# Layer 1 of a four-layer graph network: eight row steps of VectorE spread over the step, and the first product ahead of the scan

## The chip, the cores and the metric

The kernel runs on one core of one Trainium2 chip, as one launch. The metric is device time in microseconds (us), the median of three runs. The core has five engines with queues of their own: TensorE (PE in the profile, PEld for its weight loads), VectorE (DVE), ScalarE (ACT), GpSimd (POOL) and SyncE (SP, which only starts transfers). They meet at semaphores. An engine works through its queue in order, so a wait holds everything behind it on that engine.

## The reference, cut to what matters

Four graph layers run one after the other over 3125 nodes of 64 features and 100,000 edges, sorted by destination. A layer norm of the sum of input and layer output ends each of them. The change touches only the edge stage of layer 1:

```
q     = (x @ Wq)                       # nodes x 8 heads x 16
x_dst = x[edge gather]                 # 64 features per edge
k     = wk * sum_s sh[:, s] * (x_dst @ Cqk[:, s, :])     # s = 0..8
v     = wv * sum_s sh[:, s] * (x_dst @ Cv[:, s, :])
attn  = sum over 16 of q[node] * k     # 8 logits per edge
alpha = softmax of attn over the edges of one node
upd   = segment_sum(v * alpha)
```

The node of `q`, of the softmax and of the sum is the one by which the edges are sorted. The edges of one node are therefore neighbours, and softmax and sums are done as scans.

## The kernel before, in words

Each of the 128 partitions holds a run of 784 neighbouring edges, taken eight at a time (`C = 8`). So layer 1 has `NCH = 98` steps, one for each eight columns, and `edges_1` holds the queues of all engines for them. Nearly every buffer is a pair, chosen by the parity of the step. VectorE and TensorE run steps in a loop of two (`chunks`; its first four and last two steps stand outside the loop on VectorE). GpSimd, ScalarE and SyncE have all 98 steps written out (`all_chunks`). Inside the loop a semaphore is compared with a number worked out from the loop's register.

In one step t the engines do this:

- **SyncE** loads `SHB` (the factors sh, 1 MB), `SH_LAST` (512 KB), `WKV` (wk and wv, 1 MB) and `Q` (`spread_q`, 512 KB), in this order, each behind the waits that tell that its buffer is free. `Q` holds the q row only at the first edge of each node and zero elsewhere.
- **GpSimd** issues eight indirect gathers of source rows (line 1315, tile `G`), one for each column. Between columns 3 and 4 stand two tensor instructions: `messages` (line 1300, `MSG` = v times weight, for the step four earlier in its own order) and `low_part` (line 1292, `LAST`). `messages` waits for `args_ready` of the step after its own.
- **TensorE** turns the gathered rows (line 1334, `XT`; needs all eight gathers) and then makes eight columns (lines 1348 to 1352, `COLS`). Its order is column 0 of step t, the turn of step t+1, columns 1 to 7 of step t. `col_done` rises behind column 3 and behind column 7.
- **VectorE** makes from `XT` and the factors the operands `LAST` (line 1433) and `XF` (line 1435) of step t+1. `product` (line 1444) multiplies one half of `COLS` by `WKV`. `expand_q` (line 1457) fills `Q`: row j is row j of `Q` plus `SAME_HERE` times row j-1, eight dependent instructions. `ask` (line 1468) multiplies the first half of `WKV` by `Q`. `logits` (lines 1476, 796, 800, 802, 804) reduces to logits, scans the running maximum and makes the arguments of the exponentials. `sums` (line 1491) is the scan of the messages, 1224 elements long.
- **ScalarE** does the exponentials, the decay factors, the split of `LAST` in two parts (`high`, `split`) around `low_part`, and the stores of scanned rows.

VectorE's order in step t is second product of t-1, logits of t-1, LAST and XF of t+1, sums of t-2, first product of t, the eight row steps of t+1, ask of t+1.

For the operands that matter below: `XT` and `COLS` lie in PSUM, and so LAST, XF and the products read one tensor from SBUF. The row steps, ask, the maximum scan, the three argument instructions and the scan of `sums` read two tensors from SBUF. `messages` and `low_part` read two from SBUF on GpSimd.

Of the kernel before, what the change touches and what calls it, by code (L numbers as in the profile page):

```python
# [18 lines left out]
ALU = mybir.AluOpType  # L19
ACT = mybir.ActivationFunctionType  # L20
AX = mybir.AxisListType
# [6 lines left out]
C = 8  # L28
J = 784
NCH = J // C  # L30
# [3 lines left out]
CH = 16  # L34
# [21 lines left out]
def graph_kernel(nc, x, dst_shifted, src, ea16t, ea64t, ea9t, etype, ew, w64, we8, cfix, w1, w2, b1, b2, wout, vecs, basis,  # L56
# [16 lines left out]
    spread_q = dram("spread_q", [EPAD, 128])  # L73
# [10 lines left out]
    with top:  # L84
# [49 lines left out]
        class Steps:  # L134
# [10 lines left out]
            def wait(self, back=0):  # L145
                self.eng.wait_ge(self.sem, self.base + (self.n - back))
# [1078 lines left out]
        def edges_1(src_ap):  # L1225

            with ExitStack() as ctx:
                e = Edges(ctx, 1, [(x1_tab, 128, "src")], {"src": src_ap})
                WKV = e.pair("WKV", [P, C, 256])
                Q = e.pair("Q", [P, C, 128])  # L1230
                FIRST_Q = sb("FIRST_Q", [P, 128], F32, ctx)
                SRC = sb("SRC", [P, J], I32, ctx)
                SAME_HERE = e.pair("SAME_HERE", [P, C])
                SHB, XF = e.pair("SHB", [P, 4, C * P]), e.pair("XF", [P, 4, C * P])
                SH_LAST, LAST = sb("SH_LAST", [P, C * P], F32, ctx), sb("LAST", [P, C * P], F32, ctx)
                RW = e.pair("RW", [P, C, 256])
# [15 lines left out]
                asked, weighted = e.sem("asked"), e.sem("weighted")  # L1252

                with nc.Block() as block:
                    @block.sync
                    def _(sp):
                        sp.dma_start(SRC[:, :], src_ap).then_inc(src_in, 16)
                        sp.dma_start(CF[:, :, :], cfix[0:4 * P, :].rearrange("(k p) n -> p k n", p=P))\
                          .then_inc(w_in, 16)
                        sp.dma_start(CF_LAST, cfix[4 * P:5 * P, :]).then_inc(w_in, 16)  # L1260

                        def step(t, n, b, first, last):
                            if not first:
                                wait(sp, made, t * 2 - 2)
                            for h in range(2):
                                sp.dma_start(SHB[b][h:P:2, :, :].rearrange("p k n -> p (k n)"),
                                             ea9t[bass.ds(t, 1), h, 0:4 * C * P].to_broadcast([64, 4 * C * P]))\
                                  .then_inc(sh_in[b], 16)
                            if not first:
                                wait(sp, made, t * 2 - 1)  # L1270
                            sp.dma_start(SH_LAST[:, :], ea9t[bass.ds(t, 1), 0, 4 * C * P:5 * C * P]
                                         .to_broadcast([P, C * P])).then_inc(last_in, 16)
                            if not first:
                                wait(sp, col_used, t * 2 - 2)
                            sp.dma_start(WKV[b][:, :, :], row_view(wkv_tab, t)).then_inc(wkv_in[b], 16)
                            if not first:
                                wait(sp, q_expanded, t)
                                wait(sp, asked, t - 1)
                            sp.dma_start(Q[b][:, :, :], row_view(spread_q, t)).then_inc(q_in[b], 16)
                        all_chunks(step)  # L1280

                    @block.gpsimd
# [133 lines left out]
                    def _(v):  # L1416
# [8 lines left out]
                        def outer(t, n, b, first):  # L1425

                            wait(v, sh_in[b], (n + 1) * 32)
                            if not first:
# [5 lines left out]
                              .then_inc(made, 1)  # L1434
                            nc.vector.tensor_tensor(XF[b][:, 0:4, :], XT[:, :].unsqueeze(1).to_broadcast([P, 4, C * P]),  # L1435
                                                    SHB[b][:, 0:4, :], ALU.mult).then_inc(made, 1)
# [11 lines left out]
                        def expand_q(t, n, b, first):  # L1448

                            st = Steps(v, q_steps, t * (C - 1))  # L1450
                            if first:
                                wait(v, first_q_in, 16)
                            wait(v, q_in[b], (n + 1) * 16)
                            wait(v, flagged, t + 1)
                            row = FIRST_Q[:, :] if first else Q[1 - b][:, C - 1, :]
                            for j in range(C):
                                ins = nc.vector.scalar_tensor_tensor(out=Q[b][:, j, :], in0=row,  # L1457
                                                                     scalar=SAME_HERE[b][:, j:j + 1],
                                                                     in1=Q[b][:, j, :], op0=ALU.mult, op1=ALU.add)
                                row = Q[b][:, j, :]  # L1460
                                if j < C - 1:
                                    st.then(ins)
                            ins.then_inc(q_expanded, 1)

                        def ask(t, n, b):
                            wait(v, wkv_in[b], (n + 1) * 16)
# [1 line left out]
                            nc.vector.tensor_tensor(WKV[b][:, :, 0:128], WKV[b][:, :, 0:128], Q[b][:, :, :], ALU.mult)\  # L1468
                              .then_inc(asked, 1)

                        def logits(t, n, b, first):
                            st = Steps(v, e.a_steps, t * 4)
                            wait(v, col_used, (t + 1) * 2)
                            if not first:
                                wait(v, e.args_ready, t)
                            st.do(nc.vector.tensor_reduce(e.LG[:, :, 1:1 + C].rearrange("p h j -> p j h"),
                                                          RW[b][:, :, 0:128].rearrange("p j (h c) -> p j h c", c=CH),
                                                          AX.X, ALU.add))
                            wait(v, broken, t + 1)
                            e.maxima(v, st, t, n, b, first)  # L1480
                            assert st.n == 4, st.n

                        def sums(t, n, b, first):
                            wait(v, e.decays_ready, t * 2 + 2)
# [9 lines left out]
                            wait(v, e.scanned, t + 1)  # L1494

                        def step(t, n, b, first, last):
                            if first:
                                expand_q(0, 0, 0, True)
                                ask(0, 0, 0)
                                outer(0, 0, 0, True)  # L1500
# [12 lines left out]
                        end = NCH - 1  # L1513
                        product(end, NCH // 2 - 1, 1, 1)
                        logits(end, NCH // 2 - 1, 1, False)
# [490 lines left out]
```

## Time and profile before

| what | value |
|---|---|
| median of three runs | 5541.78 us |
| the three runs | 5535.75, 5542.93, 5541.78 us |
| profiled execution, its own time | 5538.3 us |
| its span | 5536.5 us |
| PE, DVE, ACT, POOL busy, share of span | 49%, 67%, 35%, 72% |
| layer 1's edge stage, steady steps | 1405.42 to 3070.77 us of the span |

The shares are means over stages of different kinds. The stretch in the last row is 92 whole steps, from the start of one LAST instruction of VectorE to that of another 92 steps later. A row of the timeline begins with start and duration in us, then engine, line, operation, output<-inputs and shapes; in brackets stand the idle time of the engine before it and what ended it. Two instructions can overlap in time on VectorE: the next may start before the recorded end of the one before.

### The profile page before, as it was taken

Reading aid. Unit: us, or ns where it says so; the run is one execution under the profiler, and the core shown is the slowest. Engines: PE = TensorE matmul, PEld = TensorE weight load, DVE = VectorE, ACT = ScalarE, POOL = GpSimd, SP = SyncE. Lnnn points to the kernel's source line nnn. Section 1 sums busy time; section 2 is a strip of 40 time slices with the busy share of each in tenths; the row PEclk is TensorE's granted clock in tenths of the full one; section 3 lists DMA queues with packets and bytes.
Section 4 is the critical chain, followed back from the end, with each engine's and each line's share of the span. In section 5 each row is a group of like instructions: output and inputs, shape, how many; then the busy total and the mean of one; then the engine's idle time right before and its main releaser. Section 6 shows DMA issues by size and latency. Waiting matters only on the chain. (4 is left out here: it accounts for less than half of the span.)

```text
span 5536.5 us, 48725 instructions
## 1 busy us (share of the span) xinstructions
PE 2686.0 (49%) x12353; PEld 2156.0 (39%) x12353; DVE 3714.6 (67%) x5208; ACT 1939.4 (35%) x3077; POOL 4005.5 (72%) x3569
## 2 busy tenths in 40 slices
PE   1777776745999999999999530000001610000001
PEld 0444444434888888888888530000000410000001
DVE  3888888864999999999999656666665532222223
ACT  0666666641333333333333222222222311111111
POOL 4777777755888888888888457777776057777774
PEclk8899989977999999999999755555555865555555
DMA  7777777745777777777778333333333632222221
GB/s 287 251 259 259 256 257 258 257 154 207 299 286 298 294 286 299 291 290 300 292 289 301 114 90 107 109 106 107 108 107 88 282 138 55 53 55 55 53 55 44
DMA packets 393535, 1064.64 MB, mean 192 GB/s; under 512 B 140390, under 2 KB 163490, under 8 KB 352228
## 3 DMA queue, kind: packets, MB, share of 16 engines
q1 hardware_dynamic: 229156, 753.21, 36.8%
q0 software_dynamic: 107840, 167.64, 11.8%
q10 hardware_dynamic: 56448, 142.93, 6.8%
q14 instruction: 76, 0.62, 0.0%
q8 instruction: 15, 0.25, 0.0%
HBM read 671.77 MB, written 391.75 MB: 192 GB/s over the span
## 5 line engine op out<-in xcount | busy, mean ns | idle before, releaser
L1348 PE MATMUL COLS<-CF,XF 128*128 128x256 f32 x6272 | 1490.2, 381 | 8.0 <-DVE XF L1435 7.5
L1348 PEld LDWEIGHTS COLS<-CF,XF 128*128 128x128 f32 x6272 | 1140.0, 191 | 131.4 <-DVE XF L1435 7.9
L1315 POOL DMA_INDIRECT G<-x_tab,SRC x784 | 1016.6, 1297 | 233.4 <-issue 203.1
L772 POOL DMA_INDIRECT G<-rel_tab,IDX_rel x784 | 739.8, 944 | 387.0 <-issue 249.0
L1615 PE MATMUL CP<-IDENT,LROW 128*68 128x128 f32 (+1 forms) x12 | 3.4, 422 | 2041.9 <-DVE SM L1736 2041.9
L772 POOL DMA_INDIRECT G<-xl_tab,IDX_src x784 | 778.1, 992 | 259.1 <-issue 249.7
L886 ACT ACTIVATE OUT<-SC 128x576 f32<-128x576 f32 (+3 forms) x392 | 572.6, 1461 | 1073.2 <-DVE SC L832 914.2
L772 POOL DMA_INDIRECT G<-kv_tab,IDX_src x784 | 739.7, 943 | 250.6 <-issue 249.7
L1615 PEld LDWEIGHTS CP<-IDENT,LROW 128*68 128x68 f32 (+1 forms) x12 | 1.5, 158 | 2042.9 <-DVE SM L1736 2042.8
L825 DVE TENSOR_TENSOR MSG<-G,EW 128x512 f32<-128x512 f32 x98 | 100.0, 1020 | 733.8 <-DMA G<-rel_tab,IDX_rel 724.6
L996 PE MATMUL WK<-W,HT 128*128 128x256 f32 x1568 | 451.0, 415 | 0.0
L1435 DVE TENSOR_TENSOR XF<-XT,SHB 128x4096 f32<-128x4096 f32 x98 | 432.7, 4415 | 0.0
L1351 PE MATMUL COLS<-CF_HI,X 128*128 128x256 f32 x784 | 366.9, 468 | 0.0
L993 PE MATMUL WK<-B2R,ONER 128*128 128x512 f32 x392 | 229.6, 586 | 271.8 <-ACT WKV L1044 270.1
L996 PEld LDWEIGHTS WK<-W,HT 128*128 128x128 f32 x1568 | 329.0, 210 | 53.7
L853 ACT ACTIVATE EX<-ARG 128x64 f32<-128x64 f32 (+1 forms) x196 | 55.5, 283 | 808.5 <-DVE ARG L804 808.5
L1491 DVE TENSOR_TENSOR_SCAN SC<-DEC,MSG 128x1224 f32<-128x1224 f32 x98 | 321.7, 3282 | 12.9 <-POOL MSG L1300 9.3
L1300 POOL TENSOR_TENSOR MSG<-RW,EX 128x1024 f32<-128x1024 f32 x98 | 284.5, 2903 | 27.1 <-DVE ARG L804 22.4
L1457 DVE SCALAR_TENSOR_TENSOR Q<-Q,SAME_HERE 128x128 f32<-128x128 f32 x783 | 274.7, 351 | 24.3
L832 DVE TENSOR_TENSOR_SCAN SC<-DEC,MSG 128x612 f32<-128x612 f32 (+1 forms) x196 | 272.6, 1391 | 14.9
L1161 DVE TENSOR_TENSOR T<-G,XE 128x512 f32<-128x512 f32 x98 | 67.4, 688 | 313.8 <-DMA G<-kv_tab,IDX_src 313.8
L1444 DVE TENSOR_TENSOR RW<-COLS,WKV 128x1024 f32<-128x1024 f32 x196 | 239.4, 1221 | 19.0 <-PE COLS L1352 7.3
(252 smaller groups left out, 5685.5 us busy)
## 6 DMA issues: line engine op xcount, KB each, us to landing
SHB<-ea9t SPq DMA_DIRECT2D x196, 1024.0 KB, 9.9
wkv_tab<-WKV SPq DMA_DIRECT2D x98, 1024.0 KB, 7.6
WKV<-wkv_tab SPq DMA_DIRECT2D x98, 1024.0 KB, 5.1
scan<-OUT ACTq DMA_DIRECT2D x196, 288.0 KB, 2.5
scan<-OUT ACTq DMA_DIRECT2D x98, 576.0 KB, 2.9
rel_tab<-YS SPq DMA_DIRECT2D x25, 2048.0 KB, 7.4
RAW<-spread SPq DMA_DIRECT2D x196, 256.0 KB
spread_q<-ZQ SPq DMA_DIRECT2D x98, 512.0 KB
```

Source lines behind the costliest of these rows:

```text
L772: pool.indirect_dma_start(out=self.G[g][b][:, c, :], out_offset=None, in_=tab, in_offset=bass.IndirectOffsetOnAxis(ap=self.IDX[which][b][: ...
L832: nc.vector.tensor_tensor_scan(flat(SC[b][:, 0:R, :]), flat(self.DEC[b][:, :, :]), flat(self.MSG[:, :, :]), 0.0, ALU.mult, ALU.add)\
L886: nc.scalar.activation(self.OUT[b][:, :, 0:WD], SC[b][:, 0:WD, 1:1 + C].rearrange("p r j -> p j r"), ACT.Copy).then_inc(self.copied_out, 1)
L996: last = nc.tensor.matmul(WK[:, 512 * i + 256 * a:512 * i + 256 * a + 256], HT[b][:, a, cc * P:(cc + 1) * P], W2[:, :], start=False, stop= ...
L1300: nc.gpsimd.tensor_tensor(e.MSG[:, 0:128, 1:1 + C].rearrange("p (h c) j -> p h c j", c=CH), RW[b][:, :, 128:256].rearrange("p j (h c) -> p ...
L1315: pool.indirect_dma_start(out=e.G[0][b][:, col, :], out_offset=None, in_=x1_tab, in_offset=bass.IndirectOffsetOnAxis(ap=SRC[:, at:at + 1], ...
L1348: nc.tensor.matmul(acc, XF[b][:, k, edges_], CF[:, k, :], start=(k == 0), stop=False)
L1351: nc.tensor.matmul(acc, X4[b][:, edges_], CF_HI[:, :], start=False, stop=False)
L1435: nc.vector.tensor_tensor(XF[b][:, 0:4, :], XT[:, :].unsqueeze(1).to_broadcast([P, 4, C * P]), SHB[b][:, 0:4, :], ALU.mult).then_inc(made, 1)
L1444: nc.vector.tensor_tensor(RW[b][:, four, :], COLS[which][:, :].rearrange("p (c n) -> p c n", c=4), WKV[b][:, four, :], ALU.mult).then_inc( ...
L1457: ins = nc.vector.scalar_tensor_tensor(out=Q[b][:, j, :], in0=row, scalar=SAME_HERE[b][:, j:j + 1], in1=Q[b][:, j, :], op0=ALU.mult, op1=A ...
L1491: nc.vector.tensor_tensor_scan(flat(SC[b][:, 0:136, :]), flat(e.DEC[b][:, :, :]), flat(e.MSG[:, :, :]), 0.0, ALU.mult, ALU.add)\
```

## The change

VectorE's instructions of layer 1 come in another order. `outer` is split in `outer_last` (LAST) and `outer` (XF). `expand_q` becomes `row_step`, of which one is called at a time, and `logits` calls a function `beside` at three places. The one-semaphore chain of `logits` becomes four semaphores. The first product stands ahead of the scan, and takes over a wait for `messages`. SyncE loads `Q` directly behind `SHB`, when row step 0 of the step before is done.

```diff
@@ sync
+                            if not first:
+                                wait(sp, q_steps, (t - 1) * (C - 1) + 1)
+                                wait(sp, asked, t - 1)
+                            sp.dma_start(Q[b][:, :, :], row_view(spread_q, t)).then_inc(q_in[b], 16)
                             if not first:
                                 wait(sp, made, t * 2 - 1)
                             sp.dma_start(SH_LAST[:, :], ea9t[bass.ds(t, 1), 0, 4 * C * P:5 * C * P]
                                          .to_broadcast([P, C * P])).then_inc(last_in, 16)
                             if not first:
                                 wait(sp, col_used, t * 2 - 2)
                             sp.dma_start(WKV[b][:, :, :], row_view(wkv_tab, t)).then_inc(wkv_in[b], 16)
-                            if not first:
-                                wait(sp, q_expanded, t)
-                                wait(sp, asked, t - 1)
-                            sp.dma_start(Q[b][:, :, :], row_view(spread_q, t)).then_inc(q_in[b], 16)
@@ vector
                             if which == 0:
                                 wait(v, asked, t + 1)
+                                if not isinstance(t, int) or t >= 2:
+                                    wait(v, weighted, t - 1)
...
+                        def row_step(t, n, b, j):
+
+                            if j == 0:
+                                wait(v, q_in[b], (n + 1) * 16)
+                                wait(v, flagged, t + 1)
...
+                                    wait(v, q_expanded, t)
+                                    row = Q[1 - b][:, C - 1, :]
+                            else:
+                                wait(v, q_steps, t * (C - 1) + j)
+                                row = Q[b][:, j - 1, :]
...
-                        def logits(t, n, b, first):
-                            st = Steps(v, e.a_steps, t * 4)
+                        def logits(t, n, b, first, beside):
...
+                                                    AX.X, ALU.add).then_inc(reduced, 1)
+                            beside(1)
+                            wait(v, reduced, t + 1)
                             wait(v, broken, t + 1)
...
+                                                         0.0, ALU.add, ALU.max).then_inc(maxed, 1)
+                            beside(2)
+                            wait(v, maxed, t + 1)
...
+                                                    ALU.subtract).then_inc(lowered, 1)
+                            beside(3)
+                            wait(v, fallen, t + 1)
+                            wait(v, lowered, t + 1)
...
                         def step(t, n, b, first, last):
+                            def row(j):
+                                if not last:
+                                    row_step(t + 1, n + b, 1 - b, j)
+
...
                                 product(t - 1, before(n, b), 1 - b, 1)
-                                logits(t - 1, before(n, b), 1 - b, isinstance(t, int) and t == 1)
+                                row(0)
+                                logits(t - 1, before(n, b), 1 - b, isinstance(t, int) and t == 1, row)
+                            row(4)
                             if not last:
-                                outer(t + 1, n + b, 1 - b, isinstance(t, int) and t == 0)
+                                outer_last(t + 1)
+                                outer(n + b, 1 - b)
+                            product(t, n, b, 0)
+                            row(5)
                             if not isinstance(t, int) or t >= 2:
                                 sums(t - 2, n - 1, b, isinstance(t, int) and t == 2)
-                            product(t, n, b, 0)
+                            row(6)
+                            row(7)
                             if not last:
-                                expand_q(t + 1, n + b, 1 - b, False)
                                 ask(t + 1, n + b, 1 - b)
```

## Rows read from the trace of the kernel before

**Rows 1.** Busy time by stretch: length, PE, PEld, DVE, ACT, POOL, PEclk, DMA share, GB/s.
```profile
1405.42:3070.77 1665.35, 1549.73 (x8097) 1380.02 (x8096) 1583.15 (x1749) 633.17 (x1012) 1442.38 (x917) 1.00 0.78 293
```
**Rows 2.** Timeline of VectorE, one step: start, duration, engine, line, operation.
```profile
2199.53 1.22 DVE L1476 TENSOR_REDUCE LG<-RW 128x64 f32<-128x1024 f32 x1
2200.88 0.31 DVE L796 TENSOR_TENSOR_SCAN SC<-BR,LG 128x72 f32<-128x72 f32 x1
2201.22 0.23 DVE L800 TENSOR_TENSOR ARG<-SC 128x64 f32<-128x64 f32 x1
2201.36 0.22 DVE L802 TENSOR_TENSOR ARG<-LG,SC 128x64 f32<-128x64 f32 x1
2201.62 0.23 DVE L804 TENSOR_TENSOR ARG<-ARG,BR 128x64 f32<-128x64 f32 x1
...
2202.09 1.23 DVE L1433 TENSOR_TENSOR LAST<-XT,SH_LAST 128x1024 f32<-128x1024 f32 x1 [0.24 <-issue]
...
2203.23 4.42 DVE L1435 TENSOR_TENSOR XF<-XT,SHB 128x4096 f32<-128x4096 f32 x1
...
2207.56 3.18 DVE L1491 TENSOR_TENSOR_SCAN SC<-DEC,MSG 128x1224 f32<-128x1224 f32 x1
...
2210.86 1.23 DVE L1444 TENSOR_TENSOR RW<-COLS,WKV 128x1024 f32<-128x1024 f32 x1
...
2212.00 3.06 DVE L1457 SCALAR_TENSOR_TENSOR Q<-Q,SAME_HERE 128x128 f32<-128x128 f32 x8
...
2215.16 1.23 DVE L1468 TENSOR_TENSOR WKV<-WKV,Q 128x1024 f32<-128x1024 f32 x1
...
2216.30 1.22 DVE L1444 TENSOR_TENSOR RW<-COLS,WKV 128x1024 f32<-128x1024 f32 x1
```
**Rows 3.** Groups of VectorE over 92 steps: xcount, busy us, mean ns, idle before.
```profile
L1491 DVE TENSOR_TENSOR_SCAN SC<-DEC,MSG 128x1224 f32<-128x1224 f32 x92 | 304.6, 3311 | 0.0
```
**Rows 4.** Timeline of GpSimd, the same step.
```profile
2202.93 2.92 POOL L1300 TENSOR_TENSOR MSG<-RW,EX 128x1024 f32<-128x1024 f32 x1
...
2205.78 2.39 POOL L1292 TENSOR_TENSOR LAST<-LAST,X 128x1024 f32<-128x1024 f32 x1
...
2208.32 3.21 POOL L1315 DMA_INDIRECT G<-x_tab,SRC  x1 [0.16 <-issue]
...
2214.34 0.94 POOL L1315 DMA_INDIRECT G<-x_tab,SRC  x1 [0.30 <-issue]
...
2215.59 1.62 POOL L1315 DMA_INDIRECT G<-x_tab,SRC  x1 [0.30 <-issue]
...
2220.01 0.94 POOL L1315 DMA_INDIRECT G<-x_tab,SRC  x1 [0.30 <-DVE ARG L804]
```
**Rows 5.** Timeline of an early step: low_part ends before the scan starts.
```profile
1373.09 2.38 POOL L1292 TENSOR_TENSOR LAST<-LAST,X 128x1024 f32<-128x1024 f32 x1
...
1375.49 2.70 DVE L1491 TENSOR_TENSOR_SCAN SC<-DEC,MSG 128x1224 f32<-128x1224 f32 x1
...
1375.61 3.38 POOL L1315 DMA_INDIRECT G<-x_tab,SRC  x1
```
**Rows 6.** Timeline of TensorE: the turn, the last matmul of columns 3 and 7.
```profile
2216.96 1.09 PE L1334 MATMUL XT<-IDENT,G 128*128 128x128 f32 x8 [1.21 <-DMA G<-x_tab,SRC]
...
2223.66 0.28 PE L1352 MATMUL COLS<-CF_LO,X 128*128 128x256 f32 x1
...
2231.51 0.28 PE L1352 MATMUL COLS<-CF_LO,X 128*128 128x256 f32 x1
```
**Rows 7.** Timeline: VectorE instructions and gathers that start close together, twice.
```profile
1362.81 0.94 POOL L1315 DMA_INDIRECT G<-x_tab,SRC  x1 [0.30 <-issue]
...
1363.23 1.22 DVE L1468 TENSOR_TENSOR WKV<-WKV,Q 128x1024 f32<-128x1024 f32 x1
...
2309.08 0.38 DVE L796 TENSOR_TENSOR_SCAN SC<-BR,LG 128x72 f32<-128x72 f32 x1
...
2309.12 0.94 POOL L1315 DMA_INDIRECT G<-x_tab,SRC  x1 [1.74 <-issue]
```
**Rows 8.** SyncE's load of Q: its issue, and over 92 steps the time to landing.
```profile
2217.99 0.35 SPq L1279 DMA_DIRECT2D Q<-spread_q  x1
...
DMA to landing us min/median/max: 5.6/6.2/6.8
```
**Rows 9.** Timeline of TensorE, two turns of early steps.
```profile
1351.69 1.04 PE L1334 MATMUL XT<-IDENT,G 128*128 128x128 f32 x8
...
1368.28 1.03 PE L1334 MATMUL XT<-IDENT,G 128*128 128x128 f32 x8
```
**Rows 10.** Timeline of VectorE in an early step, outside the loop.
```profile
1369.82 0.23 DVE L804 TENSOR_TENSOR ARG<-ARG,BR 128x64 f32<-128x64 f32 x1
1370.02 1.23 DVE L1433 TENSOR_TENSOR LAST<-XT,SH_LAST 128x1024 f32<-128x1024 f32 x1
```

More of the change, by code:

```diff
@@ L1252, in edges_1 @@
                 asked, weighted = e.sem("asked"), e.sem("weighted")
+                reduced, maxed = e.sem("reduced"), e.sem("maxed")
+                fallen, lowered = e.sem("fallen"), e.sem("lowered")
                 with nc.Block() as block:
@@ L1423, in _, with outer_last @@
                           .then_inc(cf_lo, 1)
-                        def outer(t, n, b, first):
-                            wait(v, sh_in[b], (n + 1) * 32)
-                            if not first:
+                        def outer_last(t):
+                            if not isinstance(t, int) or t > 0:
                                 wait(v, col_done, t * 2 - 2)
@@ L1434, in outer @@
                               .then_inc(made, 1)
+                        def outer(n, b):
+                            wait(v, sh_in[b], (n + 1) * 32)
                             nc.vector.tensor_tensor(XF[b][:, 0:4, :], XT[:, :].unsqueeze(1).to_broadcast([P, 4, C * P]),
@@ L1446, in product @@
                                                     WKV[b][:, four, :], ALU.mult).then_inc(col_used, 1)
[L1448 to L1463, printed above, removed]
+                        def row_step(t, n, b, j):
+                            if j == 0:
+                                wait(v, q_in[b], (n + 1) * 16)
+                                wait(v, flagged, t + 1)
+                                if isinstance(t, int) and t == 0:
+                                    wait(v, first_q_in, 16)
+                                    row = FIRST_Q[:, :]
+                                else:
+                                    wait(v, q_expanded, t)
+                                    row = Q[1 - b][:, C - 1, :]
+                            else:
+                                wait(v, q_steps, t * (C - 1) + j)
+                                row = Q[b][:, j - 1, :]
+                            nc.vector.scalar_tensor_tensor(out=Q[b][:, j, :], in0=row, scalar=SAME_HERE[b][:, j:j + 1],
+                                                           in1=Q[b][:, j, :], op0=ALU.mult, op1=ALU.add)\
+                              .then_inc(q_steps if j < C - 1 else q_expanded, 1)
                         def ask(t, n, b):
@@ L1469, in ask @@
                               .then_inc(asked, 1)
[L1471 to L1472 removed]
+                        def logits(t, n, b, first, beside):
+                            flat = lambda ap: ap.rearrange("p h j -> p (h j)")
+                            MS = e.MS[b]
                             wait(v, col_used, (t + 1) * 2)
@@ L1475, in logits @@
                                 wait(v, e.args_ready, t)
-                            st.do(nc.vector.tensor_reduce(e.LG[:, :, 1:1 + C].rearrange("p h j -> p j h"),
-                                                          RW[b][:, :, 0:128].rearrange("p j (h c) -> p j h c", c=CH),
-                                                          AX.X, ALU.add))
-                            wait(v, broken, t + 1)
-                            e.maxima(v, st, t, n, b, first)
-                            assert st.n == 4, st.n
+                            nc.vector.tensor_reduce(e.LG[:, :, 1:1 + C].rearrange("p h j -> p j h"),
+                                                    RW[b][:, :, 0:128].rearrange("p j (h c) -> p j h c", c=CH),
+                                                    AX.X, ALU.add).then_inc(reduced, 1)
+                            beside(1)
+                            wait(v, reduced, t + 1)
+                            wait(v, broken, t + 1)
+                            wait(v, e.max_carried, t)
+                            if not first:
+                                wait(v, e.copied_out, t - 1)
+                            nc.vector.tensor_tensor_scan(flat(MS[:, :, :]), flat(e.BR[:, :, :]), flat(e.LG[:, :, :]),
+                                                         0.0, ALU.add, ALU.max).then_inc(maxed, 1)
+                            beside(2)
+                            wait(v, maxed, t + 1)
+                            if not first:
+                                wait(v, e.exps_ready, t)
+                            nc.vector.tensor_tensor(e.ARG[:, 0, :, :], MS[:, :, 0:C], MS[:, :, 1:1 + C], ALU.subtract)\
+                              .then_inc(fallen, 1)
+                            nc.vector.tensor_tensor(e.ARG[:, 1, :, :], e.LG[:, :, 1:1 + C], MS[:, :, 1:1 + C],
+                                                    ALU.subtract).then_inc(lowered, 1)
+                            beside(3)
+                            wait(v, fallen, t + 1)
+                            wait(v, lowered, t + 1)
+                            nc.vector.tensor_tensor(e.ARG[:, 0, :, :], e.ARG[:, 0, :, :], e.BR[:, :, 1:1 + C], ALU.add)\
+                              .then_inc(e.args_ready, 1)
                         def sums(t, n, b, first):
@@ L1496, in step @@
                         def step(t, n, b, first, last):
+                            def row(j):
+                                if not last:
+                                    row_step(t + 1, n + b, 1 - b, j)
                             if first:
-                                expand_q(0, 0, 0, True)
+                                for j in range(C):
+                                    row_step(0, 0, 0, j)
                                 ask(0, 0, 0)
-                                outer(0, 0, 0, True)
+                                outer_last(0)
+                                outer(0, 0)
+                                for j in range(4):
+                                    row(j)
                             else:
                                 product(t - 1, before(n, b), 1 - b, 1)
-                                logits(t - 1, before(n, b), 1 - b, isinstance(t, int) and t == 1)
+                                row(0)
+                                logits(t - 1, before(n, b), 1 - b, isinstance(t, int) and t == 1, row)
+                            row(4)
                             if not last:
-                                outer(t + 1, n + b, 1 - b, isinstance(t, int) and t == 0)
+                                outer_last(t + 1)
+                                outer(n + b, 1 - b)
+                            product(t, n, b, 0)
+                            row(5)
                             if not isinstance(t, int) or t >= 2:
                                 sums(t - 2, n - 1, b, isinstance(t, int) and t == 2)
-                            product(t, n, b, 0)
+                            row(6)
+                            row(7)
                             if not last:
-                                expand_q(t + 1, n + b, 1 - b, False)
                                 ask(t + 1, n + b, 1 - b)
@@ L1514, in _ @@
                         product(end, NCH // 2 - 1, 1, 1)
-                        logits(end, NCH // 2 - 1, 1, False)
+                        logits(end, NCH // 2 - 1, 1, False, lambda j: None)
                         sums(end - 1, NCH // 2 - 1, 0, False)
```

## The prediction

> **What bounds the kernel now.** I read the busy shares first, and they name no engine: over 92 steady steps of layer 1, VectorE is busy 1583 of 1665 us, TensorE 1550, GpSimd 1442 [rows 1]. The PEclk column is 1.00 there, so TensorE's clock is at its 2.4 GHz level and no term of what follows. A step takes 1665.35 / 92 = 18.10 us.
>
> Then I laid the timelines of VectorE and GpSimd side by side, and they show a cycle through both. VectorE's scan lasts 3.18 us and ends at 2210.74, which is 2.57 behind the end of GpSimd's low_part at 2208.17 [rows 2, 4]. In an early step, where low_part had ended 0.02 before it started, the same scan took 2.70 [rows 5]. Over the 92 steps it averages 3.311 [rows 3]: it waits 0.61 each time. The reverse holds as well. The gather that starts at 2208.32 runs until 2211.53, 0.79 behind the scan's end, where other gathers take 0.94. The gather at 2215.59 ends 0.82 behind the end of ask (2216.39) [rows 2, 4]. So a scan or an ask that is running holds back a gather that starts, and a running low_part holds back the scan.
>
> GpSimd's step follows. Its own work is 0.15 from low_part to the first gather, 7 x 1.25 + 0.94 for eight gathers (0.94 and a gap of 0.30), 0.02, 2.85 from messages to low_part and 2.39 for low_part: 15.10 us. The scan adds 3.21 - 0.94 = 2.27 and ask 1.62 - 0.94 = 0.68 [rows 4]. The sum, 18.05, is the step to 0.05. TensorE isn't the limit: it waits 1.21 us a step for the last gather [rows 6], and turns 16.59 apart when nothing holds it [rows 9].
>
> **The change part by part, in time since product 1 starts.**
>
> *VectorE's path.* Dependent instructions start 0.03 to 0.10 behind the end of the one before (eight row steps take 3.06), independent ones 0.09 ahead of it (XF starts at 2203.23, LAST ends at 2203.32) [rows 2]. A row step of 0.35 therefore costs 0.38 now and 0.26 between strangers. From the reduce to LAST it is 2.56 now; in the new order the starts are 1.13, 0.26, 0.22, 0.26, 0.14, 0.14, 0.26, 0.14, 0.26 apart, 2.81 in all, with four row steps inside. New waits against register values come in: inside the loop five of them let LAST start 0.47 behind the last argument instruction [rows 2], outside it 0.20 [rows 10], about 0.05 each. In the short stretch they may push LAST by 0.1 (bounds 0 and 0.5): 2.9. Ahead of it, product to reduce is 1.40 instead of 1.26. Then LAST to XF 1.14, XF to product 0 4.33, product 0 to row 5 1.14, row 5 to scan 0.26: 11.2 from product 1 to the scan. The scan takes 2.70 if low_part is over, ask starts 0.93 behind its end (0.10 + 0.38 + 0.35 + 0.10), and the next product 1.14 later. VectorE alone would need 11.2 + 2.70 + 0.93 + 1.14 = 16.0 us, against 18.0 now.
>
> A rule of the Trainium skill speaks against this part ("VectorE: DVE Perf Modes", section "The DRAIN you can't avoid"): each instruction starts only when the pipeline has emptied, and leaving a semaphore out gains nothing. By that rule fifteen starts between product 1 and the scan would come 0.09 later each, 11.2 would be 12.55, and the loop worked out below would take 36.2 for two steps: 18.1 a step, no gain. The timeline disagrees, with XF 0.09 ahead of LAST's end; so I leave this a small part of the case "same".
>
> *TensorE.* From turn to the end of column 7 it takes 14.83 [rows 6]. Left alone it would make a step of 16.59 to 16.84 (1549.73 / 92) [rows 1, 9].
>
> *GpSimd, which decides.* Count from the end of low_part as 0. The scan now follows product 0 and row step 5. The first gather starts at 0.15. If the scan starts at 0.2 or later, that gather goes through and the second, due at 1.40, is held until 0.79 behind the scan's end at 2.90: it ends at 3.69 instead of 2.34, 1.35 late. The third starts at 4.00, inside ask (3.83 to 5.06), and ends at 5.88, another 0.94 late. Step: 15.10 + 1.35 + 0.94 = 17.39, and with the 0.05 that the sum above lacks 17.45. The other way round the loop agrees: the last gather ends at 7.13, 1.68 to the turn (2215.28 to 2216.96), 14.83 to column 7, 0.04, then VectorE's 11.2 to the scan: 34.9 for two steps, 17.44 each. VectorE then waits about 1.4 a step for column 7.
>
> Forecast: 18.10 - 17.45 = 0.65 a step, 92 steps, 60 us off the profiled execution's 5538.3 (span and 1.8 around it), which stands 3.5 below the median of the runs. That is 5478; I say **5480**.
>
> *At nothing.* Product 0's new wait for messages: messages end at 2205.85, and product 0 moves to where the scan starts now, 2207.56 [rows 2, 4], 1.7 of slack; behind it would stand row 5, the scan and ask. Column 3 is ready 6.98 behind the turn [rows 6], about then. Q's load is issued now behind WKV's, at 2217.99, lands 6.2 later and is needed at 2230 [rows 2, 8]. Afterwards it is asked for about a step sooner, behind SHB's, and needed about 17 us later. SH_LAST and WKV queue behind it on SyncE, but its wait ends with row step 0, before LAST and about when WKV's buffer is free. Without that cover every late microsecond would be one of VectorE's. The first steps and the layer's end wait for gathers and messages anyway: 0 to 5 us.
>
> **The rivals.**
>
> *Slower: the scan beats the first gather.* If row step 5 and the scan queue up behind low_part, row 5 ends at 0.22 and the scan starts at about 0.13, the gather at 0.15: a photo finish. If the scan has it, the first gather ends at 3.6, the second starts at 3.9 inside ask (3.73 to 4.96), ends at 5.78 instead of 2.34, 3.44 late: 15.10 + 3.44 + 0.05 = 18.6, since scan and ask now stand 0.93 apart where 4.4 lay between them. That is 0.5 x 92 = 46 us worse, 5584. For it: the scan that starts 0.12 ahead of a gather wins [rows 5], and the state keeps itself, since in it VectorE arrives before low_part ends. GpSimd also loses 1.4 us now and then (the idle of 1.74 ahead of one gather [rows 7]), which pushes low_part late. Against it: a scan that starts 0.04 ahead of a gather lost, taking 0.38 instead of 0.31, while the gather took its 0.94; and a gather 0.42 ahead of ask went free [rows 7]. If row steps didn't compete with low_part at all, the scan would take over at 0 and the step be about 18.3, 5560.
>
> The Trainium skill ("SBUF — State Buffer", section "Who interferes with whom") says that whichever of VectorE and GpSimd issues first keeps the shared pair for the whole instruction. It gives no order for a queue behind a third, so it supports either finish.
>
> *Faster: TensorE becomes the bound.* If the gathers slip between scan and ask, GpSimd needs under 16.84 and the step is TensorE's: 1.26 x 92 = 116, 5422. Against it: scan and ask follow each other within less than a gather and its gap (1.25), so both are hit.
>
> *Same.* Steps that alternate between the two finishes, or five short instructions in a row that hold a fourth gather back by 0.6 (17.45 + 0.6): 5535.
>
> **How the numbers follow.** Forecast 0.48, TensorE's bound 0.08, slower 0.34, same 0.10. This kernel's measurement can't tell less than 0.2%, 11 us, from nothing. Faster is 0.56, same 0.10, slower 0.34. The likeliest case alone spans 5455 to 5515 (queue waits 0 to 0.5, 17.2 to 17.85). The range reaches to the slower case and leaves TensorE's bound outside: 5440 to 5592.
>
> **What would show it right or wrong.** Right: the scan at 2.70 instead of 3.31, the first gather behind low_part at 0.94, the second at 2.3, the third at 1.9, a step of 17.4, and an idle of VectorE ahead of product 1 that ends with COLS. Slower case: the first gather at 3.5, the second at 1.9, and row step 5 far above 0.35. If Q's load is late, VectorE idles ahead of row step 0 for a DMA. If LAST starts over 0.6 behind row step 4, the waits in the queue cost more than I allow. The prediction fails if the held gathers together cost GpSimd over 2.95 a step.

## The result and the profile after

The changed kernel takes 5555.14 us, median of 14 runs (5542.88 to 5561.33); the kernel before, run beside it, takes 5543.62 (5535.75 to 5551.03). The ratio is 1.0018 with a 95% interval of 1.0009 to 1.0026: slower by 0.18%, no change by the bound of 0.2%. I had forecast 5480.

The profiled execution is the fastest of the 14: 5542.88 us, span 5541.1. Busy time by stretch over 92 whole steps of it, the columns as in [rows 1], and below that one long step:

```profile
1406.79:3074.25 1667.46, 1555.41 (x8093) 1383.01 (x8092) 1455.75 (x1749) 634.08 (x1013) 1410.58 (x916) 0.98 0.78 293
2056.60:2081.68 25.08, 17.29 (x88) 15.41 (x87) 16.60 (x20) 8.55 (x17) 22.00 (x14) 0.90 0.82 318
```

VectorE is busy 127 us less than in [rows 1], and the 92 steps take 1667.46 instead of 1665.35. Groups of VectorE over the same stretch:

```profile
L1518 DVE TENSOR_TENSOR_SCAN SC<-DEC,MSG 128x1224 f32<-128x1224 f32 x92 | 248.9, 2705 | 0.0
L1451 DVE TENSOR_TENSOR RW<-COLS,WKV 128x1024 f32<-128x1024 f32 x184 | 224.7, 1221 | 135.3 <-PE COLS L1354 127.8 <-POOL MSG L1302 6.2
...
L1434 DVE TENSOR_TENSOR LAST<-XT,SH_LAST 128x1024 f32<-128x1024 f32 x92 | 112.7, 1225 | 52.2 <-PE XT L1336 52.2
```

The scan's 3311 ns [rows 3] have become 2705. VectorE now waits 128 us for columns and 52 us for the turn. The next timelines show that these are two different things. First an ordinary step, GpSimd then VectorE:

```profile
2211.61 0.99 POOL L1317 DMA_INDIRECT G<-x_tab,SRC  x1 [0.16 <-issue]
2212.91 2.20 POOL L1317 DMA_INDIRECT G<-x_tab,SRC  x1 [0.31 <-issue]
2215.41 1.95 POOL L1317 DMA_INDIRECT G<-x_tab,SRC  x1 [0.30 <-issue]
2217.67 0.94 POOL L1317 DMA_INDIRECT G<-x_tab,SRC  x1 [0.30 <-issue]
```
```profile
2201.94 1.22 DVE L1485 TENSOR_REDUCE LG<-RW 128x64 f32<-128x1024 f32 x1
...
2204.77 1.22 DVE L1434 TENSOR_TENSOR LAST<-XT,SH_LAST 128x1024 f32<-128x1024 f32 x1
...
2211.64 2.72 DVE L1518 TENSOR_TENSOR_SCAN SC<-DEC,MSG 128x1224 f32<-128x1224 f32 x1
...
2217.98 1.22 DVE L1451 TENSOR_TENSOR RW<-COLS,WKV 128x1024 f32<-128x1024 f32 x1 [1.43 <-PE COLS L1354]
...
2222.21 1.22 DVE L1434 TENSOR_TENSOR LAST<-XT,SH_LAST 128x1024 f32<-128x1024 f32 x1
```

The step is 2222.21 - 2204.77 = 17.44. The first gather goes through, the second takes 2.20, the third 1.95, and product 1 waits 1.43. This is the forecast state, to the hundredth.

Every 14 steps something else happens, six times in all: GpSimd, VectorE, SyncE and TensorE in the long step of the windows above.

```profile
2056.54 0.94 POOL L1317 DMA_INDIRECT G<-x_tab,SRC  x1 [2.43 <-issue]
...
2062.82 2.37 POOL L1294 TENSOR_TENSOR LAST<-LAST,X 128x1024 f32<-128x1024 f32 x1
2065.35 3.41 POOL L1317 DMA_INDIRECT G<-x_tab,SRC  x1 [0.16 <-issue]
2069.06 1.91 POOL L1317 DMA_INDIRECT G<-x_tab,SRC  x1 [0.30 <-issue]
2071.28 0.95 POOL L1317 DMA_INDIRECT G<-x_tab,SRC  x1 [0.30 <-issue]
2072.53 0.94 POOL L1317 DMA_INDIRECT G<-x_tab,SRC  x1 [0.30 <-issue]
```
```profile
2063.07 1.23 DVE L1451 TENSOR_TENSOR RW<-COLS,WKV 128x1024 f32<-128x1024 f32 x1 [0.91 <-POOL MSG L1302]
2064.21 1.14 DVE L1469 SCALAR_TENSOR_TENSOR Q<-Q,SAME_HERE 128x128 f32<-128x128 f32 x1
2065.27 2.69 DVE L1518 TENSOR_TENSOR_SCAN SC<-DEC,MSG 128x1224 f32<-128x1224 f32 x1
...
2081.68 1.22 DVE L1434 TENSOR_TENSOR LAST<-XT,SH_LAST 128x1024 f32<-128x1024 f32 x1 [7.30 <-PE XT L1336]
```
```profile
2071.32 0.32 SPq L1281 DMA_DIRECT2D WKV<-wkv_tab  x1
2071.68 1.41 SPq L1268 DMA_DIRECT2D SHB<-ea9t  x2
2073.19 0.54 SPq L1274 DMA_DIRECT2D Q<-spread_q  x1
```
```profile
2079.45 1.96 PE L1336 MATMUL XT<-IDENT,G 128*128 128x128 f32 x8 [7.79 <-DMA G<-x_tab,SRC]
```

Read downwards. GpSimd pauses for 2.43 us (such pauses were there before too, at the same gathers, with 1.39 to 1.74 us of idle [rows 7]). Row step 5 is held to the end of low_part (1.14 instead of 0.34), the scan starts 0.08 ahead of the first gather and holds it: 3.41. So the fourth gather ends at 2073.47, and SyncE's loads of 2.5 MB began at 2071.32. The gather's rows land about 6.0 us later (counted to the start of the turn that waits for them), where 2.0 is usual after the change and 1.68 stood in the kernel before. TensorE waits 7.79 and VectorE 7.30. In the ordinary step the fourth gather ended about 0.7 us ahead of the loads, and in the kernel before 2.27 ahead.

The ledger over 92 steps, from the starts of LAST: 6 long steps of 25.51 on average, 6 behind them of 19.05, and 80 others of 17.50. Before, it was 6 of 19.08 at the pauses and 86 of 18.03. The ordinary steps give 80 x 0.53 = 42.6 us back. The long ones cost 6 x (25.51 - 19.08) = 38.6 more than the steps at the pauses did before, and the ones behind them 6 x (19.05 - 18.03) = 6.1: together 44.7. The sum, +2, is what the windows show.

Four of the 80 are 18.4 to 18.6 long, at distances of 17, 17 and 34 steps. In them the fourth gather ended in time, 0.6 to 0.7 us ahead of the loads, and still landed 3.2 to 3.4 later. Why is not known.

### The profile page after: what moved, and what is told of

The parts are those of the page before. It is cut to its first block and busy times, and to the rows that moved or that the text cites. A ratio compares the mean times of both kernels' runs of the same rounds, so it can differ in the third digit from the quotient of the medians.

```text
span 5541.1 us, 48688 instructions
## 1 busy us (share of the span) xinstructions
PE 2710.3 (49%) x12353; PEld 2174.2 (39%) x12353; DVE 3584.0 (65%) x5208; ACT 1941.9 (35%) x3077; POOL 3969.0 (72%) x3569
## 5 line engine op out<-in xcount | busy, mean ns | idle before, releaser
L1317 POOL DMA_INDIRECT G<-x_tab,SRC x784 | 985.7, 1257 | 239.9 <-issue 234.2
L996 PE MATMUL WK<-W,HT 128*128 128x256 f32 x1568 | 466.1, 425 | 0.0
L1518 DVE TENSOR_TENSOR_SCAN SC<-DEC,MSG 128x1224 f32<-128x1224 f32 x98 | 265.1, 2705 | 6.8 <-ACT MSG L1385 3.6
```

The source lines that it names most:

```text
L996: last = nc.tensor.matmul(WK[:, 512 * i + 256 * a:512 * i + 256 * a + 256], HT[b][:, a, cc * P:(cc + 1) * P], W2[:, :], start=False, stop= ...
L1317: pool.indirect_dma_start(out=e.G[0][b][:, col, :], out_offset=None, in_=x1_tab, in_offset=bass.IndirectOffsetOnAxis(ap=SRC[:, at:at + 1], ...
L1518: nc.vector.tensor_tensor_scan(flat(SC[b][:, 0:136, :]), flat(e.DEC[b][:, :, :]), flat(e.MSG[:, :, :]), 0.0, ALU.mult, ALU.add)\
```

## The experiments

All ratios are against the kernel before, run on the same chip beside each. Two explanations of the long steps were set against each other. Theory A says that the last gather before the turn lands late because it goes out behind SyncE's loads. Rival B says that GpSimd's pause, and the first gather that the scan then holds back, cost the time by themselves. In parentheses stand each run's name, as the expectations use it, its time, its ratio and the ratio's 95% interval.

**The loads wait for the turn** (`e1_gate`, 5521.13 us, ratio 0.9976, 0.9962 to 0.9990).

```diff
                                 wait(sp, col_used, t * 2 - 2)
+                                wait(sp, turned, t + 1)
                             sp.dma_start(WKV[b][:, :, :], row_view(wkv_tab, t))
```

> The changed kernel with one wait more: SyncE's load of WKV (and with it SHB and Q queued behind) waits until TensorE has turned the rows that these loads could overtake. Theory A (landing): the changed kernel's steady step is 0.6 us shorter, and this is lost in six stalls of about 8 us, where the last gather goes out behind SyncE's 2.5 MB and lands 6 us later instead of 2. Then the stalls vanish, each turn starts within 2 us of its last gather, and the time is about 55 us below the changed kernel's, near 5500. Rival B (hiccup): GpSimd's own pause of 2.4 us and the gather then lost to the scan cost the time, whatever the loads do. Then the six long steps stay and the time is within 5 us of the changed kernel's, 5550 to 5560.

In the 92 steady steps no turn started more than 3.1 us behind its last gather. GpSimd, VectorE and TensorE at the first pause:

```profile
1536.49 0.94 POOL L1318 DMA_INDIRECT G<-x_tab,SRC  x1 [2.62 <-issue]
...
1545.29 3.42 POOL L1318 DMA_INDIRECT G<-x_tab,SRC  x1 [0.16 <-issue]
...
1552.47 0.94 POOL L1318 DMA_INDIRECT G<-x_tab,SRC  x1 [0.30 <-issue]
```
```profile
1536.31 1.23 DVE L1435 TENSOR_TENSOR LAST<-XT,SH_LAST 128x1024 f32<-128x1024 f32 x1
...
1557.26 1.23 DVE L1435 TENSOR_TENSOR LAST<-XT,SH_LAST 128x1024 f32<-128x1024 f32 x1 [2.94 <-PE XT L1337]
```
```profile
1555.03 1.97 PE L1337 MATMUL XT<-IDENT,G 128*128 128x128 f32 x8 [3.44 <-DMA G<-x_tab,SRC]
```

The long step is 20.95; the six average 20.4 instead of 25.5. The gather before the turn lands 1.6 to 1.7 us later at all six pauses, where the changed kernel had 6.0 to 6.6: that is 4.7 of the 5.1 us. Another 0.5 is the turn itself, 1.48 on average instead of 1.96; in the changed kernel TensorE's granted clock had fallen while it waited (the last section has the rows). So theory A holds for the larger part. The pause and the gather lost to the scan keep about 3 of the 8, which is rival B's part. The time fell by less than I expected, because this kernel also fell into the forecast's slower rival for stretches. Of the eleven steps from 2707.7 to 2914.8 us of its span nine lost the first gather (3.4 us), and most of the steps there are 18.5 to 19.7 long. Its runs spread over 37 us (5505 to 5542).

**Rows spread, product behind the scan** (`e2_rows_only`, 5491.71 us, ratio 0.9924, 0.9911 to 0.9938).

```diff
-                            product(t, n, b, 0)
-                            row(5)
                             if not isinstance(t, int) or t >= 2:
                                 sums(t - 2, n - 1, b, isinstance(t, int) and t == 2)
+                            product(t, n, b, 0)
+                            row(5)
                             row(6)
```

> The changed kernel with the first product behind the scan again; the row steps stay spread and Q's early load stays. Both theories: the scan waits for low_part as before (3.2 us), always beats the first gather (3.2 us), and the step is 15.10 + 2.27 + about 0.1 to 0.2 for a gather that meets ask, 17.5. Theory A (landing): the last gather before the turn ends only about 0.4 us ahead of SyncE's loads, so each pause of GpSimd puts it behind them and stalls remain, 5540 to 5560. Rival B (hiccup, lost race): there is no race that a pause could turn over, so nothing is lost at a pause but its own 1 to 2 us, 5490.

Rival B's sentence came true: steps of 17.5 on average, six steps of 19.2 at the pauses (two of them with one of 18.9 behind), none longer. At such a pause VectorE and GpSimd look like this:

```profile
2037.52 4.66 DVE L1518 TENSOR_TENSOR_SCAN SC<-DEC,MSG 128x1224 f32<-128x1224 f32 x1 [1.01 <-POOL MSG L1302]
...
2050.05 1.22 DVE L1434 TENSOR_TENSOR LAST<-XT,SH_LAST 128x1024 f32<-128x1024 f32 x1
```
```profile
2037.24 2.37 POOL L1294 TENSOR_TENSOR LAST<-LAST,X 128x1024 f32<-128x1024 f32 x1
2039.77 3.21 POOL L1317 DMA_INDIRECT G<-x_tab,SRC  x1 [0.16 <-issue]
```

My expectation for theory A was wrong about this kernel rather than about the cause. I had taken the fourth gather to slip behind the loads when GpSimd is late. But here the scan stands directly behind XF and waits for low_part, 4.66 us at this pause, so VectorE, and with it product 1 and the loads, is late by as much. The smallest distance of the fourth gather ahead of the loads is 0.32 us in all steps, pauses included.

**Product ahead, rows in one block, Q loaded late** (`e3_product_only`, 5509.41 us, ratio 0.9956, 0.9942 to 0.9969). All eight row steps stand again between the scan and ask, and `logits` calls nothing beside itself.

> The other part alone: the first product ahead of the scan, but the eight row steps in one block ahead of ask and Q loaded where it was before. Both: scan 2.70, second gather held, step 17.3 to 17.5, because ask now stands 3.3 us behind the scan. Theory A (landing): the last gather ends about 2.4 us ahead of SyncE's loads, as in the kernel before, so a pause of GpSimd doesn't put it behind them: no stalls, about 5485. Rival B (hiccup, lost race): the scan still competes with the first gather behind low_part, a pause of GpSimd turns the race over and the long steps stay, 5530 or more.

Steps of 17.6, 19.8 at the pauses and 18.4 to 20.0 behind them, no long ones: the fourth gather is never less than 0.34 us ahead of the loads. The first gather behind low_part was lost to the scan at all six pauses (3.21), as rival B said, but no step of 25 us came of it. That is theory A's side of the question, at 24 us more than it said. Each part alone is faster than the kernel before, and both together are not.

**Q loaded where it was** (`e4_q_late`, 6047.75 us, ratio 1.0928, 1.0909 to 1.0948).

> The changed kernel with Q's load where it was before (behind WKV's, when all row steps of the step before are done). Row step 0 stands directly behind the second product, and the load is issued only when that product is done: VectorE should idle 5 to 7 us ahead of row step 0 in every step, of which the 1.4 us that it waits for TensorE now are no cover. Step about 23 us, time near 6000. If the early load didn't matter, the time would stay within 20 us of the changed kernel's.

As expected, and by a little more: VectorE idles 511 us for Q in 68 steps, 7.5 in each. So the spread rows can't be had without the early load. What the early load would bring by itself was not run. VectorE's groups in 1400 to 3000 us:

```profile
L1469 DVE SCALAR_TENSOR_TENSOR Q<-Q,SAME_HERE 128x128 f32<-128x128 f32 x544 | 188.0, 346 | 522.1 <-DMA Q<-spread_q 511.4
```

**Smaller loads** (`e5_small_loads`, 5539.55 us, ratio 1.0005, 0.9996 to 1.0015), the changed kernel with a quarter of SHB:

```diff
-                                sp.dma_start(SHB[b][h:P:2, :, :].rearrange("p k n -> p (k n)"),
-                                             ea9t[bass.ds(t, 1), h, 0:4 * C * P].to_broadcast([64, 4 * C * P]))\
+                                    sp.dma_start(SHB[b][h:P:2, 0:1, :].rearrange("p k n -> p (k n)"),
+                                                 ea9t[bass.ds(t, 1), h, 0:C * P].to_broadcast([64, C * P]))\
```

> The changed kernel, but from step 2 on SyncE loads only a quarter of SHB (256 KB instead of 1 MB); the other three quarters keep what steps 0 and 1 loaded, and so the columns are not the reference's. Nothing else moves. Theory A (landing): the last gather of a long step goes out behind 1.75 MB instead of 2.5 MB and these land sooner, so it lands after about 3.5 to 4.5 us instead of 6.3, the six long steps shrink from 25.5 to about 23, and the others keep 17.4 to 17.5: about 15 to 25 us below the changed kernel, 5535. Rival B (the pause and the lost race alone): long steps stay at 25 us, the time within 5 us of the changed kernel.

The direction is theory A's: the long steps are 24.2 to 24.7, the landing 5.1 to 5.5 us instead of 6.0 to 6.6. The ratio is 1.0005 where the changed kernel has 1.0018, some 7 us, but the two intervals overlap. The size isn't theory A's: 30% fewer bytes took only about 1.1 us off a landing. How the remaining 1.75 MB split the delay was not measured.

**The wait for the turn in the kernel before** (`e6_before_gate`, 5532.26 us, ratio 0.9990, 0.9980 to 0.9999), the one added line of the first experiment.

> The kernel before with the wait for the turn ahead of WKV's load, as in e1_gate. In it the last gather ends 2.3 us ahead of these loads and lands in 1.75 us, so there is nothing to protect. Theory A (landing): no change, within 8 us of the kernel before. Rival B' (the wait helps by spreading the loads in any case): 20 us or more faster, as e1_gate was against the changed kernel.

It is 6 us faster, within the 8 that theory A allowed and far from the rival's 20. The wait helped where gathers had slipped behind loads, and not here.

**Fewer instructions on GpSimd.** Three of the four waits of `messages` are left out but in the last three steps, once in the kernel with spread rows (`e11_rows_fewer`, 5494.50 us, ratio 0.9924, 0.9910 to 0.9937) and once in the changed kernel (`e12_fewer`, 5552.43 us, ratio 1.0023, 1.0011 to 1.0035).

> e2_rows_only, and GpSimd's messages keep only the last of their four waits (the other three are over whenever it is) but for the last three steps. If GpSimd's pause comes with the number of its instructions (some 18 a step, 15 now), it comes every 17 steps instead of every 14, five times instead of six, and as each pause costs 1.6 us here the time falls by 0 to 4 us: 5488 to 5492. If it comes with the number of gathers, the interval stays at 14 steps.

> The changed kernel with the same three waits of GpSimd's messages left out. If the pause comes with the number of instructions, the long steps come every 17 steps, five instead of six, and the time falls by about 10 us, to 5545. If it comes with the number of gathers, there are six long steps at the same places and the time stays within 5 us. In both theories a long step stays at 25 us.

In both, the six pauses came at the same gathers, 14 steps apart, and the times didn't move. So the pause doesn't follow the number of GpSimd's instructions. 14 steps are 112 gathers, and the trace of the kernel before has such a pause after every 112 gathers in the other three layers too, 142 to 149 us apart instead of 254. What it is stays open. In the second kernel two more long steps (21.7 and 22.4) away from the pauses showed that a late landing can also come without a pause. In the first of them the gather had even ended 0.10 us ahead of the loads, and landed 5.6 later. That may be why the median of the changed kernel lies 12 us above its profiled execution; a trace of a slower execution was not taken.

**low_part on VectorE.** If the coupling of two engines is the trouble, the instruction that couples them can go.

```diff
                                 outer_last(t + 1)
                                 outer(n + b, 1 - b)
+                                low_part(t + 1, 1 - b)
@@ gpsimd
-                                    if t >= 1:
-                                        low_part(t - 1, 1 - b)
```

It was tried three times: with the rows spread and the product behind the scan (`e13_low_on_vector`, 5448.46 us, ratio 0.9825, 0.9809 to 0.9841), in the changed kernel (`e14_low_product_first`, 5437.10 us, ratio 0.9810, 0.9793 to 0.9826), and in the kernel before (`e15_before_low_on_vector`, 5577.43 us, ratio 1.0067, 1.0050 to 1.0084).

> e2_rows_only with low_part moved from GpSimd to VectorE, between XF and the scan. GpSimd's step would be about 12.7 us of its own and so no longer the bound; nothing of it can hold the scan but messages, which end 1.7 us earlier. VectorE's starts add up to 1.40 + 2.83 + 1.14 + 4.33 + 1.14 (low_part) + 2.83 (scan) + 1.14 + 3 x 0.38 + 0.1 + 1.14 = 17.2 us a step, VectorE without idle. If the joint cycle of scan and low_part is what sets 17.5 in e2_rows_only and stretches at a pause, steps are 17.2, the six pauses of GpSimd cost nothing, and the time is 5455 to 5470. If something else paces it (TensorE's turn, the landings), it stays at 5490 or above.

> The changed kernel (first product ahead of the scan) with low_part moved from GpSimd to VectorE behind XF. GpSimd is then early, its last gather goes out several us ahead of SyncE's loads, and a pause doesn't push it behind them. Theory A (landing behind the loads after a pause): the six long steps of 25 us vanish altogether, steps are VectorE's 17.0 to 17.2, time 5450 to 5470. Rival: if the long steps come from VectorE's new order itself or from SyncE's new order of loads, they stay, and the time is 5500 or above.

> The kernel before, with only low_part moved from GpSimd to VectorE behind XF. VectorE then has its 18.0 us of starts, less the 0.6 that the scan waited for low_part, plus 1.14 for low_part itself: 18.5 to 18.6 a step, 40 to 50 us slower than the kernel before, near 5585. Then the spread row steps are what makes room for low_part on VectorE in e13 and e14. Rival: the move of low_part alone brings the gain of e14_low_product_first, whatever the row steps do: under 5480.

GpSimd and VectorE at a pause of the second of the three:

```profile
2004.44 0.94 POOL L1315 DMA_INDIRECT G<-x_tab,SRC  x1 [2.31 <-issue]
```
```profile
1990.63 1.23 DVE L1431 TENSOR_TENSOR LAST<-XT,SH_LAST 128x1024 f32<-128x1024 f32 x1
...
2007.72 1.22 DVE L1431 TENSOR_TENSOR LAST<-XT,SH_LAST 128x1024 f32<-128x1024 f32 x1
...
2024.86 1.23 DVE L1431 TENSOR_TENSOR LAST<-XT,SH_LAST 128x1024 f32<-128x1024 f32 x1
```

The pause of 2.31 is still there and nobody notices: 17.09 and 17.14 us for the steps around it. Every step of this kernel takes between 17.04 and 17.15 from the seventh on. Busy time by stretch of its 92 steps:

```profile
1390.94:2967.20 1576.26, 1542.51 (x8103) 1374.14 (x8102) 1552.12 (x1842) 633.66 (x1013) 1276.56 (x826) 1.00 0.83 310
```

The first two came out 7 and 13 us below the lower ends that I had given, the third 8 below 5585. VectorE is busy 1552 of 1576 us: it is the bound now. In the kernel before, the same move makes a step 18.63 (1713.51 us for 92), because VectorE has no room there. With the row steps spread, and Q's load early for them, it is 17.21. So the row steps between other instructions do pay, and they show it where VectorE alone sets the pace. The changed kernel with low_part on VectorE is the fastest of all runs here.

## Why the prediction was wrong

- **VectorE's path: right.** Reduce to LAST took 2.83 (2.81, or 2.9 with the queue's share, was said), LAST to scan 6.87 (1.14 + 4.33 + 1.14 + 0.26). Independent instructions overlap by 0.09, and row steps between them cost 0.26. The new waits in the queue cost at most 0.05 a step, not 0.1.
- **The scan: right.** 2.705 against 2.70.
- **GpSimd's sum: right for the ordinary step.** The second gather took 2.20 and the third 1.95 (2.29 and 1.88 were said), 17.44 against 17.45. Over the 80 ordinary steps, the settling behind long ones included, it was 17.50.
- **"1.68 to the turn": the step that failed.** I carried the landing time of the kernel before into an order in which the distance between the last gather and SyncE's loads shrinks from 2.27 us to about 0.7. I treated it as a constant of the loop. It was 2.0 in ordinary steps, and 6.0 to 6.6 when the gather went out behind the loads. This decided the total: with the turn at the lower clock behind it, it makes 6 x 5 of the 45 us lost at the pauses, by the first experiment. Against 17.45 in all 92 steps, the ordinary ones cost 4 us, the long ones 48 and the ones behind them 10. These 62 lead from 5480 to the profiled execution's 5542.88; the other 12 up to the median stand in no trace.
- **"GpSimd also loses 1.4 us now and then": mis-sized and misplaced.** I had it as a reason for the slower rival, priced at nothing in the forecast. After the change it lasts 2.4 (once 3.65), and it pushes low_part late, so that the scan wins over the first gather: the rest of the 45 us.
- **The slower rival: right in its mechanism, wrong in its persistence.** The photo finish is real. A queued scan starts 0.08 behind low_part's end and the gather 0.16, and the scan wins; that I had called "0.13 and 0.15", an open race. But the state didn't keep itself. VectorE stood still for the landing, GpSimd went ahead, and in the next step the scan started 2.7 to 4.0 us behind low_part's end; within three steps the kernel was back at its ordinary one. With the loads held back it did keep itself for stretches.
- **What hides Q's load: right.** No wait for Q in the changed kernel; 7.5 us a step when it is loaded late.
- **The Trainium skill's page "VectorE: DVE Perf Modes", section "The DRAIN you can't avoid",** would have given 18.1 us for every step, as I had read it. I had left out that the same section says a next instruction that isn't held starts earlier, which agrees with XF 0.09 ahead of LAST's end [rows 2]. The ordinary step shows 17.44, and the experiments show that the lack of gain comes from six steps out of 92 and not from each.
- **"Same" at 0.10** came nearest to the result, for a wrong reason: neither alternating finishes nor a fourth gather held back, but a gain of 0.53 in most steps and a loss of 7.5 at each of six pauses. That the two cancel is chance.

## What to carry to other kernels

When a change makes one engine faster, look at what its instructions release (here the second product releases 2.5 MB of loads) and how far ahead of that the slowest engine's last small transfer still is: here it shrank from 2.27 us to 0.7, and nobody had put a price on it. Count rare events of the trace before (here a pause every 14 steps) with the slack that the new order leaves them, not with the slack of the old one. And if two engines hold each other up through a shared resource, moving the coupling instruction to the engine in which room has just been made can be worth more than any order around it: 0.9810 against 1.0018.

## What the runs showed of the hardware that I had not expected

- A gather of 128 rows that ended 2.15 us behind the start of loads of 2.5 MB landed 6.0 to 6.6 us later, and 5.1 to 5.5 behind 1.75 MB. One that ended 2.27 ahead of them landed after 1.7 to 2.0, one that ended 0.5 to 0.75 ahead mostly after 2.0 to 2.2. The edge isn't sharp: one that ended 0.06 ahead took 2.9 (the changed kernel), one 0.10 ahead 5.6 (`e12_fewer`).
- Which of a VectorE scan and a GpSimd gather goes first was decided within about a tenth of a microsecond: a scan that starts 0.03 behind a gather leaves it at 0.99 us, one that starts 0.08 ahead of it makes it 3.41.
- A row step (two inputs from SBUF) that started while GpSimd's low_part ran was held to its end: 1.14 instead of 0.34.
- In every layer GpSimd pauses after each 112 gathers. In layer 1 it lasts 1.4 to 1.7 us in the kernel before and 2.4 to 3.65 after the change, in the other layers 2.0 to 4.0. It stays at the same steps with low_part gone from GpSimd (2.25 to 2.7 in `e14_low_product_first`).
- TensorE's granted clock fell in the long idle, in all six long steps: each turn behind it took 1.96 or 1.97. With idle of 2.3 to 2.5 us, at the pauses of the kernel before, it did so twice in six (1.97), and twice the turn took 1.09 as usual. In the windows below, of the changed kernel and with the columns of [rows 1], it reads 1.00, then 0.66 (a mean over 2.4 and 1.2 GHz) while TensorE waits, 0.66 in the 5 us behind it, 1.00 again. The turn took 1.96 instead of 1.09 us; the eight matmuls of the first column behind it took 3.00 us where 1.89 is usual; the next columns were 1.96 apart again.

```profile
2070.00:2075.00 5.00, 1.66 (x9) 1.30 (x7) 4.38 (x12) 1.75 (x5) 4.03 (x4) 1.00 0.80 262
2075.00:2080.00 5.00, 0.55 (x3) 0.55 (x4) 0.00 (x0) 1.04 (x5) 4.13 (x4) 0.66 1.03 418
2080.00:2085.00 5.00, 5.00 (x21) 4.39 (x20) 3.32 (x2) 1.15 (x1) 2.36 (x2) 0.66 0.88 339
2085.00:2100.00 15.00, 15.00 (x82) 13.48 (x81) 12.01 (x16) 3.96 (x4) 11.98 (x9) 1.00 0.33 98
```
